# Three of four layer norms: the per-token normalization moves from VectorE to ScalarE, as scale and bias

## The reference, cut to what matters

```
def _layernorm(x, axis=-1, eps=1e-05):
    m = jnp.mean(x, axis=axis, keepdims=True)
    v = jnp.var(x, axis=axis, keepdims=True)
    return (x - m) / jnp.sqrt(v + eps)
...
x = _layernorm(x + _L0_attn_ref(x, ...))   # Mamba-like state scan, 8 states x 256 channels   (norm 0)
x = _layernorm(x + _L0_ffn_ref(x, w))      # one 128x128 matmul with sign(w)                  (norm 1)
x = _layernorm(x + _L1_attn_ref(x, ...))   # gated linear attention, 16 heads                 (norm 2, "3" in names)
x = _layernorm(x + _L1_ffn_ref(x, ...))    # 8 experts, top 2                                 (last norm)
```

## Time and profile before

| what | value |
|---|---|
| median of 3 runs | 2474.0 us (2472.06 to 2475.73) |
| the profiled execution's own time | 2474.75 us |
| its span in the profile | 2472.9 us |
| granted TensorE clock, mean over the span | 0.951 |

### The profile page before, as it was taken

The page is one execution under the profiler, slowest core; times in us unless marked ns, Lnnn a source line. Parts: engine busy times, 40 slices in busy tenths (PEclk is TensorE's granted clock), DMA queues, the critical chain, the costliest instruction groups (busy, mean ns, idle before and its releaser), DMA issues. The chain is left out here.

```text
span 2472.9 us, 52605 instructions
## 1 busy us (share of the span) xinstructions
PE 2107.4 (85%) x15800; PEld 1560.8 (63%) x15929; DVE 1962.8 (79%) x3681; ACT 1427.6 (58%) x3256; POOL 808.0 (33%) x1060
## 2 busy tenths in 40 slices
PE   4389898989989898989898989899889849999980
PEld 1147565656657565657575656566566749999980
DVE  2787989798988888888988897989885447777768
ACT  2366766666667675666767666666655413333334
POOL 0111424141415141423324241414141333333337
PEclk9699999999999999999999999999989969999995
DMA  3452424152433324243424241524230042122117
GB/s 118 103 126 61 107 69 117 50 124 61 111 86 81 102 64 102 65 114 78 108 69 101 68 116 51 124 60 111 72 92 14 30 151 59 55 60 59 55 52 196
DMA packets 160526, 212.88 MB, mean 86 GB/s; under 512 B 20296, under 2 KB 97104, under 8 KB 160064
## 3 DMA queue, kind: packets, MB, share of 16 engines
q1 hardware_dynamic: 138192, 144.20, 19.7%
q0 software_dynamic: 22272, 67.92, 13.4%
HBM read 134.71 MB, written 28.08 MB: 66 GB/s over the span
## 5 line engine op out<-in xcount | busy, mean ns | idle before, releaser
L1432 DVE TENSOR_TENSOR_SCAN hs<-decay,push 128x512 f32<-128x512 f32 x256 | 320.1, 1272 | 7.1
L1184 ACT ACTIVATE S<-banks,fall_tok 128x128 f32<-128x128 f32 x1024 | 278.8, 385 | 27.7 <-PE banks L816 27.4
L1003 PE MATMUL banks<-rowsT,w_here 128*128 128x128 f32 x2176 | 269.6, 278 | 6.5 <-DVE w_here L1774 6.5
L1003 PEld LDWEIGHTS banks<-rowsT,w_here 128*128 128x128 f32 x2176 | 256.0, 193 | 10.1 <-issue 9.1
L1853 POOL DMA_DIRECT2D y<-ch x96 | 88.1, 918 | 477.2 <-DVE ch L1440 374.5
L1944 POOL TENSOR_TENSOR qd<-q,q_fall 128x512 f32<-128x512 f32 x96 | 159.4, 1660 | 208.7 <-ACT chunk_fall L1169 208.7
L1540 DVE TENSOR_TENSOR S<-banks,S 128x512 f32<-128x512 f32 x256 | 167.8, 683 | 64.2 <-PE banks L828 44.9
L1985 POOL DMA_INDIRECT results_scratch<-rows_out,result_to x136 | 132.2, 972 | 241.2 <-ACT rows_out L1310 234.5
L1425 DVE TENSOR_TENSOR push<-du,b_all 128x1024 f32<-128x1024 f32 x128 | 198.1, 1547 | 2.0 <-DMA b_all<-bc_scratch 2.0
L1299 ACT ACTIVATE tanh_h<-banks 128x512 f32<-128x512 f32 x136 | 81.3, 598 | 203.3 <-PE banks L1003 203.3
L1547 DVE SCALAR_TENSOR_TENSOR oT<-tog,banks 128x512 f32<-128x512 f32 x128 | 87.2, 681 | 136.0 <-ACT sq L1152 135.9
(11 more groups left out here) (221 smaller groups left out, 5096.5 us busy)
## 6 DMA issues: line engine op xcount, KB each, us to landing
y<-ch POOLq DMA_DIRECT2D x96, 512.0 KB, 5.5
b_all<-bc_scratch SPq DMA_DIRECT2D x128, 256.0 KB, 3.9
c_all<-bc_scratch SPq DMA_DIRECT2D x128, 256.0 KB, 3.6
q_fall<-fall_scratch SPq DMA_DIRECT2D x192, 128.0 KB, 3.3
rows_in<-rows_scratch SPq DMA_DIRECT2D x136, 66.0 KB
both<-results_scratch SPq DMA_DIRECT2D x32, 256.0 KB, 3.4
w<-w_dram SPq DMA_DIRECT2D x3, 2048.0 KB, 9.6
x_tok<-x_dram SPq DMA_DIRECT2D x16, 256.0 KB, 3.2
```

The source lines that it names most:

```text
L1003: mm = pe.matmul(bank_h[:, u % 2, n, here], w_here[:, u % 2, n, here], x, start=True, stop=True)
L1184: ins = nc.scalar.activation(S[:, g, here], bank[:, here], ACT.Exp, bias=fall_tok[:, head:head + 1])
L1432: nc.vector.tensor_tensor_scan(hs[:, h, :], decay[:, n % 2, h, :], push[:, h, :], 0.0, ALU.mult, ALU.add).then_inc(s_scan, 1)
```

## The change

ACT normalizes instead of DVE: `Identity` with scale = rstd and bias = shift, both per token. For that `deviation` multiplies the sum of means by -0.5 instead of 0.5, and `scale_of` on POOL has a second instruction, shift = -mean * rstd, behind a wait for its own rstd. rstd and shift become buffers with a slot per norm. The four instructions of each norm leave DVE's order and stand in ACT's: norm 0 in stage 5 behind `front(6)`, ahead of stage 6's `squares(5)`; norm 1 in stage 7 behind `squares(6)`, ahead of `squares(7)`; norm 2 in unit 2 behind the tanh of g, ahead of `state_decay` for the third scan and of unit 3. As mean is now read by POOL, `deviation` of norms 0 and 1 gets a wait for the shift of the norm before it, and `scale_of` one for the normalization of the round before.

```
-        rstd = sb_kept("rstd", [P, TILES])
+        rstd = sb_kept("rstd", [P, 3, TILES])
+        shift = sb_kept("shift", [P, 3, TILES])
...
+            def normalize(x, n, ready, done, it):
+
+                act.wait_ge(ready, at(it, 1, 1))
+                for t in range(TILES):
+                    nc.scalar.activation(x[:, t, :], x[:, t, :], ACT.Identity, bias=shift[:, n, t:t + 1],
+                                         scale=rstd[:, n, t:t + 1]).then_inc(done, 1)
...
                 if i is not None:
                     if h + 1 in STATE_IN_STAGE:
                         state_decay(STATE_IN_STAGE[h + 1], i)
+                    if h == NORM_STAGE:
+                        normalize(x1, 0, s_shift0, s_x1, i)
                     if h == STATE_OUT["x1T"]:
                         turn_mixed(i)
+                    if h == NORM2_STAGE:
+                        normalize(x2_new, 1, s_shift1, s_x2, i)
...
                 if u == 0:
                     take_mixed(TILES - 1, j, it)
+                if u == 2:
+                    normalize(x3, 2, s_shift3, s_x3, j)
...
-            def deviation(x, step, it):
+            def deviation(x, step, it, shifted=None):
+
+                if shifted is not None:
+                    dve.wait_ge(*shifted)
...
-                nc.vector.tensor_scalar(mean[:], mean[:], 0.5, None, ALU.mult).then_inc(step, 1)
+                nc.vector.tensor_scalar(mean[:], mean[:], -0.5, None, ALU.mult).then_inc(step, 1)
...
-            def normalize(x, scale, done, it):
-
-
-                dve.wait_ge(scale, at(it, 1, 1))
-                for t in range(TILES):
-                    nc.vector.tensor_scalar(x[:, t, :], x[:, t, :], mean[:, t:t + 1], rstd[:, t:t + 1],
-                                            ALU.subtract, ALU.mult).then_inc(done, 1)
...
-                deviation(x1, s_ln0, i)
+                deviation(x1, s_ln0, i, (s_shift1, at(i, 1, 0)) if not first(i) else None)
...
-                deviation(x2_new, s_ln1, i)
+                deviation(x2_new, s_ln1, i, (s_shift0, at(i, 1, 1)))
...
-            def scale_of(step, scale, it):
+            def scale_of(n, step, shifted, done, it):
 
                 pool.wait_ge(step, at(it, LN_STEPS, LN_STEPS))
-                nc.gpsimd.tensor_tensor(rstd[:], var[:], minus_half[:], ALU.pow).then_inc(scale, 1)
+                after(pool, done, at(it, TILES, 0))
+                nc.gpsimd.tensor_tensor(rstd[:, n], var[:], minus_half[:], ALU.pow).then_inc(s_scale[n], 1)
+                pool.wait_ge(s_scale[n], at(it, 1, 1))
+                nc.gpsimd.tensor_tensor(shift[:, n], mean[:], rstd[:, n], ALU.mult).then_inc(shifted, 1)
```

More of the change, by code:

```diff
@@ L474, in build @@
         s_ln3 = sem("ln3_steps")
-        s_rstd0 = sem("ln0_scale")
+        s_scale = [sem(f"ln{n}_scale") for n in (0, 1, 3)]
+        s_shift0 = sem("ln0_shift")
         s_rms_eps = sem("rms_eps_added")
-        s_rstd1 = sem("ln1_scale")
-        s_rstd3 = sem("ln3_scale")
+        s_shift1 = sem("ln1_shift")
+        s_shift3 = sem("ln3_shift")
         s_x3 = sem("x3_ready")
@@ L1402, in deviation @@
                 nc.vector.tensor_scalar(var[:], var[:], 1 / P, LN_EPS, ALU.mult, ALU.add).then_inc(step, 1)
-            def normalize(x, scale, done, it):
-                dve.wait_ge(scale, at(it, 1, 1))
-                for t in range(TILES):
-                    nc.vector.tensor_scalar(x[:, t, :], x[:, t, :], mean[:, t:t + 1], rstd[:, t:t + 1],
-                                            ALU.subtract, ALU.mult).then_inc(done, 1)
-            def layer_norm(x, step, scale, done, it):
-                deviation(x, step, it)
-                normalize(x, scale, done, it)
             def state_part(n, part, i):
@@ L1618, in stage @@
                         add_mixed(i)
-                    if h == NORM_STAGE:
-                        normalize(x1, s_rstd0, s_x1, i)
                 if n is not None:
@@ L1627, in stage @@
                         add_ffn(i)
-                    if h == NORM2_STAGE:
-                        normalize(x2_new, s_rstd1, s_x2, i)
                 if n is not None:
@@ L1644, in closing @@
                     deviation(x3, s_ln3, j)
-                if u == 2:
-                    normalize(x3, s_rstd3, s_x3, j)
                 if u == 5:
@@ L1929, in closing @@
                 if u == 1:
-                    scale_of(s_ln3, s_rstd3, j)
+                    scale_of(2, s_ln3, s_shift3, s_x3, j)
                 if u == 7:
@@ L1959, in stage @@
                     if h == MIX_STAGE:
-                        scale_of(s_ln0, s_rstd0, i)
+                        scale_of(0, s_ln0, s_shift0, s_x1, i)
                     if h == FFN_STAGE:
-                        scale_of(s_ln1, s_rstd1, i)
+                        scale_of(1, s_ln1, s_shift1, s_x2, i)
             def body(i, j, n):
```

## The result

The changed kernel took 2481.7 us (median of 16 runs, 2467.8 to 2493.7) beside 2470.5 us for the kernel before (16 runs, 2461.7 to 2477.0). The ratio is **1.0037, 95% interval 1.0024 to 1.0051: slower by some 9 us** (the two medians lie 11.2 apart), where 7 us less was forecast. The profiled execution took 2478.96 us with a span of 2477.1, against 2474.75 and 2472.9 before, so it shows 4.2 of the 9 us.

The account below looks back on a forecast made before the run. PE's work plus its waits was taken to bound the rounds, with DVE's queue late in the units. Terms of -5.3 and a clock share of -1.5 made -7 in all: 2467 us median, range 2455 to 2480, likeliest case 2458 to 2473.

Parts of the forecast that it names:

- The sum: Whole kernel before the clock: thirteen full rounds -7.8, round before +0.4, first +3.0, draining -1.7, last norm 2 +0.8: together -5.3.
- 0.4 late: Behind norm 1: PE begins x_new's transposes 0.4 us later than before, and x2T comes 0.4 late.
- three signs: Rounds: wrong if PE's wait for k of unit 5 stays, x1T costs over 1.2, or the clock's share leaves 0.98.
- Rival 1: Rounds: the 1.95 wait at x1T brings a 1.2 GHz stretch in most rounds, old ones stay; about 2488; chance 0.16.
- Rival 2: Norms: their own longer chain sets the beat, not DVE's queue; up to +2.8 a round, half gives 2495; chance 0.05.
- x1T: Norm 0: ACT's copy of x1T comes 1.2 us later, PE's wait of 0.75 becomes 1.95.
- of the 1.2 lost, 0.8 is given back: Norm 1: PE begins only 0.4 us later than before, its wait for x_new shrinking from 1.01 to 0.2.
- x3 and the units: Norm 2 and behind: x3 +1.2 (wait 2.1), unit 5's k wait of 1.62 gone, unit 7's 1.47 becomes 0.85.
- A full round: Each full round: +1.2 at x1T, -0.8 at x_new, +1.2 at x3, -1.6 and -0.6 at k, together -0.6.
- nearly the same number: Stretches at 1.2 GHz over thirteen rounds: about as many, slightly less harm, -0.1 a round, -1.5 in all.
- rival 4: Rounds: the 1.2 GHz stretches mostly go as the x_new and one k wait go; 20 less, 2454; chance 0.13.
- The ends: Outside the full rounds: first round with a norm +3.0, draining round -1.7, last norm 2 +0.8.

Follow-up runs that it names:

- shifted: Changed kernel with 48 semaphore increments heading ACT's program, moving its loop from instruction 281 to 329: 2440.8 us, ratio 0.9858 to the kernel before.
- Norm 1 alone: Kernel before with only norm 1 moved to ACT, ACT's loop at instruction 333: 2458.0 us, ratio 0.9934 to the kernel before.
- norm 0 alone: Kernel before with only norm 0 moved to ACT, ACT's loop at instruction 333: 2474.9 us, ratio 1.0016 to the kernel before.
- the two shifted kernels before: Kernel before with 30 or 64 semaphore increments heading ACT's program, loop at instruction 295 or 329, no norm moved: ratio 1.0117 or 1.0004 to the kernel before.
- norms 1 and 2: Changed kernel with norm 0 back on DVE, ACT's loop at instruction 329 by 56 increments: 2429.5 us, ratio 0.9817 to the kernel before.
- the eleven loops: ACT's loops in all eleven looped kernels: bad at instructions 281 to 582, 295 to 584 (2505.2 us) and 313 to 614 (2481.3 us), the others good.
- 64 increments: Kernel before with 64 semaphore increments heading ACT's program, loop from instruction 329 to 618, no norm moved: ratio 1.0004 to the kernel before.
- norm 2 alone: Kernel before with only norm 2 moved to ACT, ACT's loop at instruction 329: 2451.9 us, ratio 0.9912 to the kernel before.

## Why the prediction was wrong

**What failed.** The sum ("Together -5.3") has no term for the 12 instructions that the change adds to ACT's loop as code. The steps take the next round's opening as following PE alone (x2T "0.4 late"). In fact x2T came 2 us late in 12 of 13 rounds: PE waits 2.4 to 2.9 instead of 0.68. That costs 23.2 us directly and some 17 more in stretches at 1.2 GHz (23.4 against 6.2). None of the four rivals names it, and none of the three signs that the prediction gave of being wrong appeared: the wait for k of unit 5 went, x1T cost less than 1.2, and the clock's share in the rounds stayed at 0.98. Rival 1 has the sign and the mechanism of the 17 us, but puts the cause in the wait for x1T; shifted, that wait is as long (1.7) and the stretches are few. Rival 2, where the Trainium skill's rule on adds and multiplies would lead, is refuted for norms 1 and 2; for norm 0 its sign is right in the full-clock round (+0.68).

**x1T.** +1.2 forecast, +0.93 measured (0.75 to 1.68).

**x_new.** 1.01 to 0.2, as forecast, by the chain that was forecast: the norm follows ACT's sq, and sq follows PE. But it gives nothing back of norm 0's delay, as "of the 1.2 lost, 0.8 is given back" reads. Norm 1 alone, with no delay at x1T, has the same 0.19, and norm 0 alone keeps 1.00.

**x3 and the units.** Against the earlier trace rows: with the loop well placed, x3 +1.3 (+1.2 forecast); the 1.62 for k of the fifth unit gone, as forecast; k of the seventh 1.01 (0.85 forecast). In rounds behind a late branch x3 is 1.46 and the seventh 1.47: of the late 2 us, 0.8 is made up at x3 and 0.5 lost again.

**A full round.** -0.6 forecast; 113.87 against 115.04 is -1.17 with the loop well placed, -1.02 in the one round of the changed kernel without a branch ahead (114.02). The five waits of the sum came out well: +0.93 - 0.81 + 1.31 - 1.62 - 0.46 = -0.65. PE's idle time as a whole fell by 0.84 (115.04 - 103.89 to 113.87 - 103.56), its busy time by 0.33, which I had not counted. DVE's busy time fell by 3.5 a round (99.75 to 96.22), not by 4.3.

**The clock.** I took "nearly the same number" of stretches, -1.5 us in all. With the loop well placed 18.4 of 24.6 us go, where executions of the same work lay some 5 apart; my rival 4 (-15) had this at a chance of 0.13.

**The ends.** The first round with a norm: +3.0 forecast for its place, where the start as a whole is 6.0 later. ACT stood in softplus's exponentials until 123.66, as argued, and PE waited 6.91 for x1 and 3.41 for x_new:

```profile
125.34 1.11 PE L732 MATMUL banks<-eye,x 128*128 128x128 f32 x4 [6.91 <-ACT x L1104]
134.82 0.47 PE L732 MATMUL banks<-eye,x_new 128*128 128x128 f32 x1 [3.41 <-ACT x_new L1104]
```

The same moment is at 129.1 to 131.0 in the two shifted kernels before, so some 4 to 6 of it belong to the change. The draining round gave 7.8 where 1.7 was forecast; before it ran at a granted clock of 0.93 and now at 0.97. Its time goes with how much of it runs at 1.2 GHz: 114.64 with 17.1 us at that clock before, 113.25 with 13.7 (norm 0 alone), 111.60 with 13.7 (norms 1 and 2), 108.41 with 6.8 (norm 1 alone), 106.83 with 6.8 now. Work and clock were not taken apart.

**The ledger** of the changed kernel, us against before: 13 full-clock rounds -15.2, stretches -18.4, late branches +23.2, stretches that these bring +17.2, start and the round behind it +6.5, draining round -7.8, all behind it -1.2: +4.3, against 4.2 between the spans. The first two are what the shifted kernel has against before.

## What to carry to other kernels

An edit to a loop body is also an edit to its length and its place in the engine's program. Where an engine's loop has between 257 and 512 instructions (here 289 and 301; the two lines of 256 are the Trainium skill's, cited above), count both, and look in the new profile for idle time that ends on "issue" behind the back branch and for instruction packets inside the loop; a few do-nothing instructions under a wait at the head, or writing the loop out, take it away. A change that mixes several like moves should be priced and run one by one: here two of three moves give 1.8% and the third takes 0.4% back, and the change as a whole shows neither.

## What the runs showed of the hardware that was not expected

- ACT's back branch takes 0.24 to 0.27 us when its loop is well placed and 2.4 to 3.6 us when not, with 5 packets of 8 KB a round. Streaming twelve times the code cost nothing that could be measured (0.9993, 0.9978 to 1.0008). The Trainium skill's rule on a branch out of the two lines, cited above, agrees with which of the eleven loops were late.
- The waits of 2.4 us and more for x2T cost more than themselves: stretches of 3.4 and 6.8 us at 0.50 of 2.4 GHz follow in 6 of the 12 rounds, and a round with two of the longer ones took 122.16 us against 115.80.
- The stretches depend on the pattern of PE's waits in a way that no single wait explains: of 15 in 13 rounds (12 in the same kernel with 64 increments) norm 1 alone leaves 12, norm 2 alone 8, both 5, and norm 0 alone, with longer waits than before, in one profile also 5. Those at a round's opening went where PE's wait for x_new fell from 1.0 to 0.2 us.
